# A scan's carried state is added to column 0 of its input, with a new order of work on every engine

## The reference

```python
dA = jnp.exp(delta[..., None] * A)                  # 192 channels, 16 states
dBu = delta[..., None] * Bm[:, :, None, :] * u[..., None]
def step(h, inp):
    dA_t, dBu_t, C_t = inp
    h = dA_t * h + dBu_t
    y = jnp.einsum('ben,bn->be', h, C_t)
    return (h, y)
```

## Time and profile before

| | |
|---|---|
| median of 2 runs | 2520.38 us (2520.23 to 2520.53) |
| profiled execution | 2531.32 us |
| its span, first to last instruction | 2529.5 us |
| mean granted TensorE clock | 0.963 of full speed |
| busy share VectorE, GpSimd, ScalarE, TensorE | 97%, 95%, 92%, 84% |
| chunk of scans, median of 63 | 37.54 us from first scan to first scan |

### The profile page before, as it was taken

One profiled execution on the slowest core, in us unless ns is written; L12 is line 12 of the kernel. 1 busy time (PEld: TensorE's weight loads), 2 busy tenths in 40 slices (PEclk: granted clock), 3 DMA queues, 4 the chain that ended last, 5 costly groups with the idle time before them and its releaser, 6 DMA issues.

```text
span 2529.5 us, 34487 instructions
## 1 busy us (share of the span) xinstructions
PE 2129.8 (84%) x10022; PEld 790.6 (31%) x10022; DVE 2458.5 (97%) x2390; ACT 2316.7 (92%) x3960; POOL 2414.4 (95%) x718
## 2 busy tenths in 40 slices
PE   6787888888888888888888888888888888888877
PEld 3223323233333333323333323323323333333323
DVE  7999999999999999999999999999999999999986
ACT  5677777999999999999999999999999999999977
POOL 4999999999999999999999999999999999999981
PEclk8788878999999999999999999999999999999979
DMA  6555554555665665665656656656565566566533
GB/s 241 188 184 162 198 177 161 201 203 198 211 211 189 218 212 184 216 210 191 219 199 198 215 196 205 208 202 210 198 210 210 195 212 202 183 215 206 174 123 85
DMA packets 171162, 494.51 MB, mean 195 GB/s; under 512 B 23040, under 2 KB 44672, under 8 KB 154016
## 3 DMA queue, kind: packets, MB, share of 16 engines
q1 hardware_dynamic: 170976, 492.30, 57.8%
HBM read 400.33 MB, written 91.88 MB: 195 GB/s over the span
## 4 chain that ended last, share of the span: by engine, by line
DVE 69%; issue 11%; POOL 8%; PE 7%; ACT 4%; DMA 1%; DVEq 0%; SPq 0%; POOLq 0%; ACTq 0%
DVE R L1204 52%; DVE D L1188 10%; POOL R L666 6%; PE G L1428 2%; POOL D L645 2%; ACT DA L828 1%; DVE q L1284 1%; DVE G L1229 1%; DVE dl L1214 1%; PE G L1462 1%; DVE yv L1225 1%; PE Y L1505 1%; PE G L1465 1%; DVE th L1237 1%; DMA R<-ths 1%
## 5 line engine op out<-in xcount | busy, mean ns | idle before, releaser
L1204 DVE TENSOR_TENSOR_SCAN R<-DA,R,D 128x512 f32<-128x512 f32 x1344 | 1627.6, 1257 | 4.5 <-ACT DA L828 4.5
L666 POOL TENSOR_TENSOR R<-R,Cs 128x2048 f32<-128x2048 f32 x383 | 1452.7, 3815 | 2.0 <-DVE R L1204 2.0
L828 ACT ACTIVATE DA<-ds,kept_w 128x512 f32<-128x512 f32 x1536 | 1054.4, 688 | 143.4 <-DVE R L1204 129.3
L645 POOL TENSOR_TENSOR D<-us,Bs 128x2048 f32<-128x2048 f32 x193 | 736.7, 3817 | 9.6 <-DMA us<-lo_d 9.4
L1188 DVE TENSOR_TENSOR D<-us,PB 128x2048 f32<-128x2048 f32 x191 | 357.8, 1874 | 6.9 <-DMA us<-lo_d 6.9
L1462 PE MATMUL G<-un,wcv 96*128 96x512 f32 x512 | 262.4, 637 | 29.4 <-ACT h L895 29.4
L1505 PE MATMUL Y<-R,kept_w 128*32 128x512 f32 x2048 | 267.7, 618 | 8.9 <-POOL R L666 8.9
L1204 DVE TENSOR_TENSOR_SCAN R<-DA,D 128x512 f32<-128x512 f32 x192 | 221.8, 1204 | 3.3 <-ACT DA L828 3.3
L1465 PE MATMUL G<-un,wcv 96*64 96x256 f32 x1024 | 148.7, 415 | 60.3 <-ACT xq L876 59.1
L1428 PE MATMUL G<-st,kept_w 128*64 128x256 f32 (+1 forms) x384 | 113.3, 502 | 66.2 <-ACT st L790 66.2
L1428 PE MATMUL G<-sq,kept_w 96*96 96x512 f32 (+1 forms) x256 | 143.7, 645 | 23.9 <-DVE dl L1214 20.9
(11 more groups left out here) (231 smaller groups left out, 3227.6 us busy)
## 6 DMA issues: line engine op xcount, KB each, us to landing
Bs<-bc_d SPq DMA_DIRECT2D x128, 512.0 KB, 5.4
us<-lo_d SPq DMA_DIRECT2D x64, 1024.0 KB, 6.6
ds<-lo_d SPq DMA_DIRECT2D x64, 1024.0 KB, 8.5
Cs<-bc_d SPq DMA_DIRECT2D x128, 512.0 KB, 4.8
us<-hi_d SPq DMA_DIRECT2D x64, 512.0 KB, 6.9
ds<-hi_d SPq DMA_DIRECT2D x64, 512.0 KB, 5.4
lo_d<-dl SPq DMA_DIRECT2D x64, 256.0 KB, 2.0
lo_d<-du SPq DMA_DIRECT2D x64, 256.0 KB, 2.0
```

The lines of the kernel that those rows point to most:

```text
L645: nc.gpsimd.tensor_tensor(shaped(D[:, s % NDBU, :, :], s), low(us, s) if s in LOWS else high(us), of_states(Bs, s), ALU.mult).then_inc(don ...
L666: nc.gpsimd.tensor_tensor(shaped(R[:, s, :, 0:T], s), shaped(R[:, s, :, 1:S], s), of_states(Cs, s), ALU.mult).then_inc(hc_done.sem, 1)
L828: nc.scalar.activation(DA[j % NDA][:, :], ds[:, i, :], ACT.Exp, scale=A[:, j:j + 1]).then_inc(exp_done.sem, 1)
L1204: nc.vector.tensor_tensor_scan(R[:, s, q, 1:S], DA[j % NDA][:, :], D[:, s % NDBU, q, :], before, ALU.mult, ALU.add).then_inc(scanned.sem, 1)
```

## The change

In place of a first state read from R, each scan starts from the constant 0, and what the carried state adds to the first position, exp(A * delta_0) * h, is added to column 0 of the scan's input D. For the 56 chunks that go on from another (`goes_on`), VectorE gets nine small instructions, all TENSOR_TENSOR: `first_decay` makes A * delta_0 for quads 0 to 3 (16 columns) and for quads 4 and 5 (8 columns) into a new tensor E; `carry` multiplies E by R's last column (16 and 8 columns); `start` adds E to column 0 of D, once for each of quads 0 to 3 (4 columns) and once for quads 4 and 5 together (8 columns). Between `first_decay` and `carry` ScalarE takes the exponential of E, two small instructions. A, ds, R, D and E all lie in SBUF. The scans of a quad wait for its `start`, `carry` for ScalarE's exponential, `start` for `carry` and for the quad's input.

`SPLIT` goes from 240 to 320: VectorE makes 80 more columns of each of the four blocks of quad 3, GpSimd 80 fewer, and ScalarE copies 80 more columns of B. The steps of all engines except SyncE are listed in a new order, the PSUM banks G0 to G3 are handed out anew, and FRONT follows this. In the diff the first `first_decay` is ScalarE's, the second VectorE's, and `parts_of` gives E, A and column 0 of ds.

```diff
-SPLIT = {3: 240}
+SPLIT = {3: 320}
+        E = sb("E", [128, BLOCKS])
...
+            def first_decay(k, n):
+                act.wait_ge(carry_log.sem, carry_log.at(k, n + 1))
+                blocks = slice(0, 4 * QUAD) if n == 0 else slice(4 * QUAD, BLOCKS)
+                nc.scalar.activation(E[:, blocks], E[:, blocks], ACT.Exp).then_inc(carry_exp.sem, 1)
...
                     dve.wait_ge(summed.sem, summed.at(k - 1, s + 1))
-                before = 0.0 if place(k) == 0 else R[:, s, q, T:S]
-                nc.vector.tensor_tensor_scan(R[:, s, q, 1:S], DA[j % NDA][:, :], D[:, s % NDBU, q, :], before,
+                    if goes_on(k):
+                        dve.wait_ge(started.sem, started.at(k, min(s, 4) + 1))
+                nc.vector.tensor_tensor_scan(R[:, s, q, 1:S], DA[j % NDA][:, :], D[:, s % NDBU, q, :], 0.0,
                                              ALU.mult, ALU.add).then_inc(scanned.sem, 1)
...
+            def first_decay(k, n):
+                dve.wait_ge(d_in[n], count(k, 16, 16))
+                to, by, delta_0 = parts_of(n)
+                nc.vector.tensor_tensor(to, by, delta_0, ALU.mult).then_inc(carry_log.sem, 1)
+
+            def carry(k, n):
+                dve.wait_ge(carry_exp.sem, carry_exp.at(k, n + 1))
+                dve.wait_ge(scanned.sem, scanned.at(k - 1, QUAD * (4, 6)[n]))
+                quads = slice(0, 4) if n == 0 else slice(4, QUADS)
+                e = E[:, QUAD * quads.start:QUAD * quads.stop].rearrange("p (s q) -> p s q", q=QUAD)
+                nc.vector.tensor_tensor(e, e, R[:, quads, :, T], ALU.mult).then_inc(carry_in.sem, 1)
+
+            def start(k, s):
+                dve.wait_ge(carry_in.sem, carry_in.at(k, 2 if s > 3 else 1))
...
+                if s > 3:
+                    first, e = D[:, 4 % NDBU:5 % NDBU + 1, :, 0], E[:, 4 * QUAD:].rearrange("p (s q) -> p s q", q=QUAD)
+                else:
+                    first, e = D[:, s % NDBU, :, 0], E[:, QUAD * s:QUAD * s + QUAD]
+                nc.vector.tensor_tensor(first, first, e, ALU.add).then_inc(started.sem, 1)
```

More of the change, by code:

```diff
@@ L110, in inside, with goes_on @@
             return 0 <= k <= LAST - CH - OVER
+        def goes_on(k):
+            return there(k) and place(k) > 0
         def later(k):
@@ L933, in iteration @@
                     decay(g, 0, 3)
+                if there(g - 2):
+                    token_copy(g - 2, G3)
+                if place(g + 3) == 0 and later(g + 3):
+                    group_square(g + 3, PB, 1)
+                if there(g):
                     decay(g, 1, 0)
@@ L1026, in iteration @@
                     inv_ln(g - 1, 1, G2)
-                if inside(g - 10):
-                    hidden_bias(g - 10, 1)
-                    hidden(g - 10, 2, G2)
                 if there(g):
                     decay(g, 5, 2)
+                if goes_on(g + 1):
+                    first_decay(g + 1, 0)
                 if inside(g - 10):
-                    hidden_bias(g - 10, 2)
-                if place(g + 3) == 0 and later(g + 3):
-                    group_scale(g + 3, PB, 3)
+                    hidden(g - 10, 2, G2)
+                    hidden_bias(g - 10, 1)
                 if there(g):
@@ L1293, in iteration @@
                     scan(g, 0, 0)
+                if place(g + 3) == 0 and later(g + 3):
+                    aggregate(g + 3)
                 if there(g - 1):
@@ L1297, in iteration @@
                     token_norm(g - 2, G0)
-                if place(g + 3) == 0 and later(g + 3):
-                    aggregate(g + 3)
                 if there(g):
+                    inputs(g, 1)
                     scan(g, 0, 1)
-                    inputs(g, 1)
                     scan(g, 0, 2)
-                if there(g - 1):
-                    gate(g - 1, 1)
+                if goes_on(g):
+                    start(g, 1)
                 if place(g - 10) == 0 and early(g - 10):
-                    fold(g - 10, 4, G1)
+                    fold(g - 10, 4, G2)
+                if goes_on(g):
+                    start(g, 2)
                 if there(g):
@@ L1311, in iteration @@
                     scan(g, 1, 1)
+                if there(g - 2):
+                    gram(g - 2, G3)
+                if there(g):
                     scan(g, 1, 2)
-                if there(g - 2):
-                    gram(g - 2, G2)
+                if goes_on(g):
+                    first_decay(g, 1)
                 if there(g):
                     scan(g, 1, 3)
+                if there(g - 1):
+                    gate(g - 1, 1)
+                if there(g):
                     scan(g, 2, 0)
+                if there(g + 1):
+                    delta(g + 1, *((G3, G0) if g < 0 else (G1, G2)))
+                if there(g):
                     scan(g, 2, 1)
-                if there(g + 1):
-                    delta(g + 1, *((G3, G0) if g < 0 else (G0, G3)))
-                if there(g):
                     scan(g, 2, 2)
+                    scan(g, 2, 3)
                     inputs(g, 3)
-                    scan(g, 2, 3)
+                if place(g - 9) == 0 and early(g - 9):
+                    fold(g - 9, 1, G1)
+                if goes_on(g):
+                    carry(g, 1)
+                    start(g, 3)
                 if there(g - 1):
-                    scale_out(g - 1, G1)
+                    scale_out(g - 1, G0)
                 if there(g):
@@ L1681, in iteration @@
                     group_centre(g + 3, PB)
+                if inside(g - 12):
+                    x2_plain(g - 12, G0)
+                if there(g - 2):
+                    freed(silued, g + 1, 1)
+                    to_tokens(g - 2, G3)
+                if place(g - 10) == 0 and early(g - 10):
+                    freed(silued, g + 1, 3)
+                    fold(g - 10, 4, G2)
+                if inside(g - 12):
+                    x2_feed(g - 12, G0)
                 if there(g + 1):
@@ new lines, in iteration @@
+                if there(g + 1):
+                    freed(st_done, g + 1)
+                    dt_proj(g + 1, 0, G1)
+                    (freed(f_y16, g - 11) or (place(g - 10) == 0 and freed(fold_ev, g - 10, 4))
+                     or freed(silued, g + 1, 3))
+                    dt_proj(g + 1, 1, G2)
+                if there(g - 1):
+                    sum_states(g - 1, 5)
+                if inside(g - 10):
+                    (freed(post_dve, g - 2) or freed(post_act, g - 2, 5) or freed(silued, g + 1, 1))
+                    centre_tokens(g - 10, G3)
```

263 lines of the change are left out of this document (133 added, 130 removed).

## The result

The changed kernel takes 3080.33 us (3078.54 to 3082.12, 2 runs) against 2520.38: a ratio of 1.2202, 95% interval 1.2171 to 1.2232. It is slower by 560 us; 3065 was forecast.

A forecast was written before the change was run, and what follows sets the result against it. VectorE, GpSimd and ScalarE were taken as level, with anything added to VectorE's queue paid in full. A batch of 368.8 us against 300.7, +68.1, times 8 is +545, on the median 2520.38 giving 3065 us; range 2835 to 3400.

The forecast's parts named there:

- The mechanism: VectorE's nine SBUF-only instructions each wait for GpSimd's current instruction to end: 10.1 us a chunk, 3065 us, chance 0.52.
- The walk of the two queues: VectorE's and GpSimd's queues laid side by side through one chunk: 47.3 us, 10.1 of them waits, in place of 37.54.
- `start` of quad 3, which needs the result of `carry`, finds it there: 3.8 us: After `carry` in quad 3, `start` meets GpSimd's product 1 already running and waits 3.8 us, to 27.3 in the chunk.
- `start` of quads 4 and 5 is free: After three scans, at 31.3 us in the chunk, product 2 has ended and product 3 needs a scan: no wait.
- only one wait at each place: Rival: `start` of quad 3 gets in before product 1, 3.75 us a chunk less, -210 us: 2855 us, chance 0.14.
- Chunks and batches: A batch is 39.3 + 6 x 47.3 + 44.2, plus 1.5 for folds: 368.8 us against 300.7.
- Scans: VectorE's scans from a constant take 0.055 us less each, 24 times a chunk: -1.3 us in each of 56 chunks.
- The split: Split 320 in quad 3: VectorE +0.34 us a chunk, GpSimd -0.57, ScalarE's longer copy under 0.1.
- The new order of both is then covered: ScalarE has 47.3 us a chunk for 37.3 of work, GpSimd for 36.9, so their new order is hidden.
- The no-wait rival: None of the nine VectorE instructions waits for GpSimd: about -1.5 us a batch, 2508 us, 2460 to 2560, chance 0.20.

The follow-up runs named there:

- moved: The changed kernel with `start` of quads 4 and 5 moved behind L1344 and `first_decay` of quads 0 to 3 ahead of quad 4's last scan: 2897.68 us.
- psum_in: The changed kernel with each of the nine small instructions taking its second input from PSUM bank DA (carried state wrong): 2625.56 us, ratio 1.0378.
- one_col: The changed kernel with the nine as TENSOR_SCALAR on one SBUF input and a single column, ScalarE's two exponentials also one column: 2582.03 us, ratio 1.0225.
- before_320: The kernel before with the split at 320 in place of 240 and nothing else: 2542.81 us, ratio 1.0069.
- old_carry_240: The changed kernel's new order with the old way of carrying the state, no small instructions, split back at 240: 2567.84 us, ratio 1.0164 to the kernel before.
- old_carry: The changed kernel's order, banks and split of 320, state read by the scan as before, without the nine and ScalarE's two small instructions: 2606.13 us, ratio 1.0316.
- one_in: The changed kernel with each of the nine as a TENSOR_SCALAR reading one SBUF tensor of the same shape (carried state wrong): 3089.03 us, ratio 1.2216.
- beside: The changed kernel with `start` of quads 4 and 5 moved directly behind `start` of quad 3: 3245.68 us, ratio 1.2868.
- no_start45: The changed kernel without `start` of quads 4 and 5 (their carried state left out): 3041.45 us, ratio 1.2044.

## Why the prediction was right

**The mechanism.** It named the nine small instructions, held by GpSimd until the instruction in flight ends, as the whole loss. The ends of GpSimd's instructions show the holds, and moved shows that their length is what GpSimd has left. They are 9.9 us in the chunk shown, some 554 us in 56; taking them away gives back 455 us (psum_in) to 498 (one_col), since waits that they covered come up. The reason given (SBUF alone in and out, as L1400) was near enough for all nine but is narrowed by one_col; the second input in SBUF is enough, and so are several columns in a TENSOR_SCALAR. L1400 has one SBUF input, so the earlier trace rows bore on instructions with two by likeness only, and L1394 overlapped GpSimd's instruction by no more than 0.22 us, which is little to tell PSUM from SBUF by; psum_in is what shows it.

**The walk of the two queues.** Forecast chunk 47.3 us, measured 47.1 (47.12 in the one shown). By steps: `start` of quad 1 held 0.9 (1.0), of quad 2 free (free), `first_decay` 0.3 (0.4), `carry` 2.4 (2.5), `first_decay` of the next chunk 2.7 (2.7), the last `carry` and `start` free (0.17 us each). Two steps failed and cancelled: "`start` of quad 3, which needs the result of `carry`, finds it there: 3.8 us" and "`start` of quads 4 and 5 is free". In fact the first passes free behind `carry`, VectorE comes to the second 3.6 us earlier, and it meets product 2 in flight: 3.4 us. The sum is the same because both ways end with product 2, GpSimd's two products running one behind the other: a hold of 3.8 and three scans, or three scans and a hold of 3.4. That the chunk came out right to 0.2 us is in this part luck, for the prediction had the wrong instruction held. The rival *only one wait at each place* had the turn of `start` right and its price of -210 us wrong, for it left the later holds as they were.

**Chunks and batches.** A batch's first chunk was to take 39.3 us and its last 44.2; they take about 40.6 and 45.5, and the second and sixth 48.6. In the first and sixth the trace shows scans of quads 0 and 1 waiting some 1 us for ScalarE. From the third batch on a batch takes some 372.1 us where 368.8 was forecast; the first two grow by less, 60 and 64 us in place of 68. Between the profiled executions the change costs 551 us (3082.12 less 2531.32), against a forecast of 545. The other 9 of the 560 are no cost of the change: the profiled execution of before lies 11 us over its median and that of the changed kernel 2 over its own. As to the 37.54 us of before, that is the plain chunk, as the fourth or eighth of a batch; the median of all 63 distances is 37.64.

**The other terms.** Scans: a mean duration of 1202 against 1257 ns in the chunks that go on, 0.055 us less as forecast, which over 1344 scans is 74 us. The split: 93.2 against 71.7 us on VectorE, and before_320 costs 17 us by its ratio. "The new order of both is then covered" held: the scans wait only 23 us for decays in the changed kernel.

**The no-wait rival.** Its 2508 us, 2460 to 2560, was mis-sized: without holds the change takes 2626 (psum_in) or 2582 us (one_col). It summed busy time and took three full engines as a bound; old_carry_240 shows that the order alone costs 1.6%, in waits of scans for decays that no sum of busy time contains. It also put TensorE's clock at no price. Had the holds not been there, the forecast of that case would have failed.

**What stays open.** Split and order together cost more than apart (3.2% against 2.3%), and the traces show where: the waits of the second and third scan of quad 4 grow from 20 us in old_carry_240 to 35 in old_carry, and the chunks with TensorE mostly at 1.2 GHz before the third from 18 to 35. What makes the clock fall in one chunk and not in the next is open: in the 4.2 us up to 1059.20, where it fell in old_carry, TensorE was busy for 2.48 us, and in the same 4.2 us of work two chunks later, where it did not fall, for 2.48 as well. No run sets the clock and changes nothing else, so its share is read from traces alone. No run here beats the kernel before.

## What to carry to other kernels

Before a short VectorE instruction is put beside a busy GpSimd, look at where its inputs lie: with both in SBUF its price is what GpSimd's current instruction has left, here up to 3.5 us for eight columns. It can be placed where GpSimd must wait for VectorE anyway, or given one input from PSUM. And where engines run level, a hold taken out is not time won, until the trace shows who was catching up behind it; here that was ScalarE, behind a TensorE at half its clock.

## What the runs showed of the hardware

- A held VectorE instruction is recorded as busy from its turn to GpSimd's end plus some 0.03 us, so the busy share of 97% did not move while VectorE stood still for a fifth of a chunk (9.9 of 47.12 us).
- The instruction that is ready right behind a held one isn't held again (0.15 us), though GpSimd's next starts in the same instant; that product is hardly delayed (3.84 us in the chunk shown, 3.82 in the median of 56, against 3.81).
- A TENSOR_SCALAR of one SBUF column runs in 0.14 us beside GpSimd and one of eight columns takes 3.54, the hold included (one_col, one_in).
- TensorE's mean granted clock fell from 0.963 to 0.818 of full speed in the changed kernel, in which TensorE has more idle time; psum_in is at 0.93, beside at 0.81. The mean of one 96x512 group of its products (L1508, L1428 before) went from 649 to 744 ns. In the changed kernel hardly a wait of VectorE follows from that; in no_start45, beside and old_carry the waits of scans in quad 4 do, and but for 0.7 us in beside they come only where the clock was mostly at 1.2 GHz.
